# Two-layer block on one core: feed-forward weights of layer 1 in two transfers, the first feed-forward half ahead of the first value product, one pair of unread products moved

## The chip, the cores and the metric

The kernel runs on one core of one Trainium2 chip. The metric is the device time of one execution in microseconds; three executions of the kernel before took 355.24, 355.36 and 355.60 us, median 355.36.

## The reference

The input `x` is eight sequences of 256 tokens with 128 features, all float32. Two layers are computed, each as "normalise, then add an attention-like part and a feed-forward part".

```
xn = layernorm(x)
x  = x + attention0(xn) + moe0(xn)       # the change touches only this line
xn = layernorm(x)
x  = x + ssm1(xn) + ffn1(xn)
```

`attention0` has 16 query heads and 4 key/value heads of width 8, softmax over 256 keys, and an output product. `moe0` has eight logits per token (`xs @ Wg`); softmax, best two, weights divided by their sum. All experts share one pair of weights, so what is left is one gate number times `relu(xn @ w1) @ w2`, with `w1` 128x512 and `w2` 512x128. `ssm1` has an input product, a causal convolution of four taps, a gated scan over 16 states, and an output product. `ffn1` is a gated feed-forward net with two hidden 512x512 products.

The title's "layer 1" is the first of the two layers, which the code calls `layer0`.

## The kernel before

Every tensor stays in on-chip memory, 128 features or 128 tokens across the partitions. A batch is one sequence of 256 tokens, so there are eight batches in the first layer. The second layer works on four groups of 512 tokens.

Each of the five engines has a list of named steps written out by hand (`ORDERS`, line 72). The n-th occurrence of a name is the n-th call of the function of that name (`run_order`, line 127). An engine executes its list strictly in order; where a step needs something from another engine, it waits on a semaphore (`wait_ge`). Nothing reorders the steps at run time, so the place of a name in the string is the schedule.

Steps that matter here, with their lines:

- SyncE issues the transfers. At the start: `x_in` (line 361, three parts of `x`: 2, 6 and 8 tiles of 128 tokens), `head` (identity and query/key weights), `constants0` (output, value and gate weights, biases; called `cst`), `ffn_weights` (line 371, `w1` and `w2` side by side in the tile `w12`, 512 KB, one transfer). Then `put` and `put_keys` write query and key parts to DRAM, and `fetch` and `stack` read them back in another layout.
- TensorE: `xn_transposes` (line 502) turns a normalised batch, `project` (line 518) makes queries, and for the first batch a wide form of the keys, `project_keys` (line 525) makes keys, `v_gate` (line 493) makes values and gate logits, `ffn_in` (line 450) makes one half of the hidden layer of one batch (two 128-column blocks of `w1`, two steps per batch), `ffn_out` (line 464) multiplies the hidden layer with `w2`, `S` (line 381) makes scores for the row maxima, `A` makes the transposed scores for the softmax. A float32 product is recorded as two matmuls.
- `warm` (line 510) is a pair of bfloat16 products whose result nothing reads. There are 16 such pairs. They write to a bank that is otherwise unused then.
- ScalarE: `normalised` (line 553) scales `x`; `xn_out` (line 568) copies the transposed batch out of the accumulator bank, `own_keys` (line 612) masks the wide keys for the first four `S` steps; `relu` (line 579) empties an `ffn_in` bank.
- VectorE: `first_split` (line 758) cuts the first queries and keys into bfloat16 parts, `v_out` (line 698) empties the value product, `moments` (line 648) and `inverse` make the statistics, `M` (line 675) is the row maximum of one score step.

`v_gate` waits for the constants, for the transposed batch and for whatever last used its bank. For batch 0 that is written `q0` in `V_AFTER` (line 146): the query copy, the first part of `first_split`, and the wide query copy. `ffn_in` for batch 0 waits only for its weights and for the transposed batch (`-` in `F_AFTER`, line 150). It writes to a bank of its own, `bP`.

On TensorE the first steps stand in this order: eight `warm`, `xn_transposes`, two `warm`, `project`, `project_keys`, `warm`, `v_gate`, `ffn_in`, `xn_transposes`, `S`, `warm`, two `xn_transposes`, `S`, `project_keys`, `project`, two `S`, `ffn_in`, three `S`.

Of the kernel before, what the change touches and what calls it, by code (L numbers as in the profile page):

```python
# [27 lines left out]
DFF = 512  # L28
# [29 lines left out]
def reached(eng, sem, b, per, k):  # L58

    v = b * per + k  # L60
    if isinstance(v, int) and v <= 0:
        return
    eng.wait_ge(sem, v)


def settled(eng, sem, v):
# [3 lines left out]


ORDERS = dict(
    sync="""x_in head x_in constants0 x_in ffn_weights 2*put put_keys put 2*put_keys fetch 2*put_keys 2*put put_keys
        put fetch stack 3*put 3*rows stack fetch put_keys 2*put 2*rows put rows fetch 2*put put_keys loads stack
        2*rows put rows put_keys loads fetch stack 2*put 2*rows put rows fetch 3*put stack 3*rows fetch stack 2*put
        rows put 2*rows loads stack fetch 6*rows loads 3*b_rows out b_rows 7*out landed""",
    tensor="""8*warm xn_transposes 2*warm project project_keys warm v_gate ffn_in xn_transposes S warm 2*xn_transposes
        S project_keys project 2*S ffn_in 3*S 2*warm xn_transposes warm 3*S ffn_out S project 3*S ffn_in 2*S
        xn_transposes ffn_in max_rows 3*S v_gate warm 2*S ffn_out 2*S xn_transposes A S A S xn_transposes A S A S A
        project_keys S 2*A S project A S A 2*S ffn_in A S A S max_rows A S ffn_in v_gate A 2*S A S ffn_out A S project  # L80
        A S A S A S 2*pv A S A S A S pv A S A S A S pv A S A S max_rows heads A S A S v_gate pv A S A S back pv
# [77 lines left out]
def layer0(nc, sb, sem, banks, a, w, t, done):  # L159
# [11 lines left out]
    w12 = sb("w12", [P, 2 * DFF])  # L171
# [35 lines left out]

    X_PARTS = ((0, TPB), (TPB, 4 * TPB), (4 * TPB, NT))
    ld_x = [sem(f"ld_x{k}") for k in range(len(X_PARTS))]
    ld_head, ld_cst, ld_ffn = (sem(n) for n in ("ld_head", "ld_cst", "ld_ffn"))  # L210
    warm_end = sem("warm_end")
    spark_ok, warm_ok, kx_ok, own_ok, sc0_ok = (
        sem(n) for n in ("spark_ok", "warm_ok", "kx_ok", "own_ok", "sc0_ok"))
# [52 lines left out]
    def emptied(eng, before, n):  # L266

        name = before.split()[n]
        if name == "-":
            return  # L270
        for signal, per in EMPTIED[name[0]]:
            eng.wait_ge(signal, per * (int(name[1:]) + 1))
        if name == "q0":
            eng.wait_ge(q_split, 1)
            eng.wait_ge(qa_ok, 1)
# [7 lines left out]
    def sync_pieces(eng):  # L283
# [85 lines left out]
            eng.dma_start(cst[:, :], a["cst"]).then_inc(ld_cst, 16)  # L369

        def ffn_weights(n):
            eng.dma_start(w12[:, :], a["w12"]).then_inc(ld_ffn, 16)

        return dict(x_in=x_in, head=head, constants0=constants0, ffn_weights=ffn_weights, put=put, put_keys=put_keys, fetch=fetch, rows=rows,
                    stack=stack, loads=loads)


    def tensor_pieces(eng):
# [71 lines left out]
        def ffn_in(n):  # L450
            b, half = n // 2, n % 2
            if half == 0:
                eng.wait_ge(ld_ffn, 16)
                reached(eng, xnT_ok, b, 1, 1)
                emptied(eng, F_AFTER, b)
            else:
                reached(eng, h_ok, b, 2, 1)
            for j in range(2):
                c = 2 * half + j
                last = mm(bP[:, j * T:(j + 1) * T], w1[:, c * P:(c + 1) * P], xnT[b],  # L460
                          start=True, stop=True)
            last.then_inc(h_ps, 1)

        def ffn_out(b):
            reached(eng, h_ok, b, 2, 2)
            for q in range(TPB):
                for c in range(KC):
                    last = mm(bP[:, q * P:(q + 1) * P], hT[:, c, q * P:(q + 1) * P], w2[:, c, :],  # L468
                              start=(c == 0), stop=(c == KC - 1))
            last.then_inc(f_ps, 1)  # L470
# [54 lines left out]
        def project_keys(j):  # L525
# [6 lines left out]
            for i, b in enumerate(KEYS[j]):  # L532
                last = mm(key_bank(j)[32 * i:32 * i + 32, :], wk4[:, 0:NKV * HD], xnT[b], start=True, stop=True)
            last.then_inc(k_ps, 1)

        return dict(S=scores, A=attend_scores, pv=pv, heads=heads, ffn_in=ffn_in, ffn_out=ffn_out, back=back,
                    proj_out=proj_out, max_rows=max_rows, v_gate=v_gate, xn_transposes=xn_transposes,
                    project=project, project_keys=project_keys, warm=warm)
# [866 lines left out]
def program(nc, w, scr, out):  # L1405
    ctx = ExitStack()
    with ctx:
# [26 lines left out]
        with ExitStack() as only0:  # L1434
            pieces0 = layer0(nc, lambda name, shape, dt=F32: only0.enter_context(
                nc.sbuf_tensor(name, shape, dt)), sem, banks, a, w, t, done)
# [62 lines left out]
```

## Time and profile before

| quantity | value |
|---|---|
| three executions | 355.24, 355.36, 355.60 us, median 355.36 |
| the profiled execution | 355.43 us, of which the span is 353.6 us |
| TensorE busy | 343.7 us, 97% of the span |
| VectorE busy | 308.0 us, 87% |
| ScalarE busy | 287.8 us, 81% |
| GpSimd busy | 232.9 us, 66% |

The span reaches from the first to the last instruction of the five engines; 1.83 us of the profiled execution lie around it. Names in the rows: PE is TensorE, PEld its weight loads, DVE is VectorE, ACT is ScalarE, POOL is GpSimd, SPq is the queue of SyncE. L460 is line 460 of the kernel before. A row of the timeline gives start and length in microseconds, then engine, line, operation, operands, and how many instructions are merged in it. The bracket at the end is the idle time ahead of it and what ended that.

### The profile page before, as it was taken

How to read it: one execution, taken by the hardware profiler on the slowest of the kernel's cores; microseconds unless marked ns; L12 is line 12 of the kernel's file. 1: busy time of each engine (PE TensorE's matmuls, PEld its weight loads, DVE VectorE, ACT ScalarE, POOL GpSimd, SP SyncE). 2: the span in 40 equal slices, each digit the busy share in tenths (PEclk: the TensorE clock that was granted, in tenths of full speed). 3: DMA queues.
4: the chain of work that ended last, by engine and by line, in shares of the span. 5: the costliest groups of instructions: out<-in, count | busy, mean ns of one | idle time of the engine just before them, and what ended most of it. 6: DMA issues, size and time to landing. Idle time of an engine off the chain costs nothing.

```text
span 353.6 us, 5743 instructions
## 1 busy us (share of the span) xinstructions
PE 343.7 (97%) x1754; PEld 179.2 (51%) x1754; DVE 308.0 (87%) x530; ACT 287.8 (81%) x503; POOL 232.9 (66%) x294
## 2 busy tenths in 40 slices
PE   7999999999999999999999999999999999999996
PEld 4565634747565434434344446544455544555546
DVE  6899989989799798499999999999998978999840
ACT  3955886978688785899899969998999999689920
POOL 3553482332720201346997979999999989999990
PEclk9999999999999999999999999999999999999999
DMA  6449477936447003000000000000000000000000
GB/s 228 114 124 184 84 200 172 157 91 135 93 136 123 4 2 122 22 1 2 22 0 3 1 0 24 0 15 2 0 13 26 1 30 2 1 0 1 2 30 30
DMA packets 29198, 19.39 MB, mean 55 GB/s; under 512 B 4256, under 2 KB 28144, under 8 KB 28912
## 3 DMA queue, kind: packets, MB, share of 16 engines
q1 hardware_dynamic: 29168, 19.03, 22.4%
q8 instruction: 14, 0.23, 0.3%
q14 instruction: 16, 0.13, 0.1%
HBM read 13.45 MB, written 5.37 MB: 53 GB/s over the span
## 4 chain that ended last, share of the span: by engine, by line
PE 87%; DVE 6%; ACT 3%; issue 2%; POOL 1%; ACTq 0%; DVEq 0%; POOLq 0%
PE bank L1027 16%; PE bank L1016 15%; PE bank L436 7%; PE bank L423 4%; PE bank L1098 4%; PE bank L1051 4%; DVE mx L681 4%; PE bank L460 4%; PE bank L990 4%; PE bank L1071 4%; PE bank L468 4%; PE bank L1006 4%; PE bank L1007 4%; PE bank L400 3%; PE bank L1088 2%
## 5 line engine op out<-in xcount | busy, mean ns | idle before, releaser
L1367 POOL TENSOR_TENSOR acc<-acc,hb 128x512 f32<-128x512 f32 x128 | 158.3, 1267 | 16.5 <-DVE hb L1311 16.4
L1311 DVE TENSOR_TENSOR_SCAN hb<-da,bank 128x512 f32<-128x512 f32 x128 | 146.0, 1201 | 8.7 <-PE bank L990 8.1
L681 DVE TENSOR_REDUCE mx<-bank 128x2 f32<-128x512 f32 x128 | 81.6, 681 | 7.3 <-PE bank L400 4.8
L1216 ACT ACTIVATE da<-dt,nega 128x510 f32<-128x510 f32 x128 | 81.3, 709 | 0.1
L1016 PE MATMUL bank<-sil,ld 128*128 128x512 f32 x128 | 59.2, 592 | 0.0
L1027 PE MATMUL bank<-gelu,ld 128*128 128x512 f32 x128 | 58.4, 592 | 0.0
L631 ACT ACTIVATE pt<-bank 128x512 f32<-128x512 f32 x72 | 39.8, 599 | 7.0 <-PE bank L436 4.2
L423 PE MATMUL bank<-q_st,k_st 51*128 51x512 bf16 (+1 forms) x128 | 38.8, 381 | 0.5 <-ACT pt L631 0.5
L400 PE MATMUL bank<-k_st,q_st 48*128 48x256 bf16 x248 | 38.1, 272 | 0.3 <-DVE mx L681 0.2
L1027 PEld LDWEIGHTS bank<-gelu,ld 128*128 128x128 f32 x128 | 24.1, 190 | 26.0 <-issue 25.2
L1016 PEld LDWEIGHTS bank<-sil,ld 128*128 128x128 f32 x128 | 23.9, 190 | 23.2 <-issue 22.2
L631 ACT ACTIVATE hb<-bank 128x512 f32<-128x512 f32 x56 | 30.8, 595 | 5.1 <-PE bank L423 4.9
L990 PE MATMUL bank<-b_parts,sel 96*128 96x512 bf16 x64 | 23.4, 381 | 0.3 <-DVE hb L1311 0.3
L400 PEld LDWEIGHTS bank<-k_st,q_st 48*128 48x128 bf16 x248 | 17.6, 94 | 8.6 <-DVE mx L681 4.5
L423 PEld LDWEIGHTS bank<-q_st,k_st 51*128 51x128 bf16 (+1 forms) x128 | 9.2, 94 | 25.0 <-ACT pt L631 13.8
L846 POOL TENSOR_TENSOR m_parts<-negm,m_parts 32x128 bf16<-32x128 f32 x8 | 3.3, 417 | 24.9 <-ACT negm L577 24.9
L1098 PEld LDWEIGHTS bank<-ld,gelu 128*128 128x128 f32 x128 | 16.4, 192 | 4.5 <-issue 4.2
L1280 DVE SCALAR_TENSOR_TENSOR xc<-bank,ld,xc 128x510 f32<-128x510 f32 (+2 forms) x24 | 17.7, 741 | 0.7
L436 PE MATMUL bank<-pt,v_sb 128*32 128x512 f32 x144 | 17.9, 600 | 0.2 <-issue 0.2
L460 PE MATMUL bank<-xnT,w 128*128 128x256 f32 x64 | 17.5, 396 | 0.4 <-DVE on L693 0.4
L1204 ACT ACTIVATE gelu<-bank,ld 128x512 f32<-128x512 f32 x14 | 9.1, 687 | 9.4 <-PE bank L1027 9.4
L1006 PE MATMUL bank<-xnT,ld 128*128 128x512 f32 x32 | 16.5, 598 | 0.2 <-DVE mx L681 0.2
(166 smaller groups left out, 537.7 us busy)
## 6 DMA issues: line engine op xcount, KB each, us to landing
q_st<-q_scr SPq DMA_DIRECT2D x15, 192.0 KB, 3.8
q_st<-q_scr SPq DMA_DIRECT2D x7, 384.0 KB, 5.0
ld<-in_pack SPq DMA_DIRECT2D x2, 1024.0 KB, 5.6
q_scr<-qk_parts SPq DMA_DIRECT2D x8, 192.0 KB, 2.6
k_st<-k_scr SPq DMA_DIRECT2D x14, 96.0 KB, 4.7
q_scr<-qk_parts SPq DMA_DIRECT2D x8, 128.0 KB, 1.8
out<-x SPq DMA_DIRECT2D x8, 128.0 KB, 1.9
ld<-in_pack SPq DMA_DIRECT2D x1, 968.0 KB, 6.0
```

The costliest lines, as they stand in the source:

```text
L400: last = mm(score_bank(b, n)[:, j * T:(j + 1) * T], q_st[b % 2][0:ROWS, 2 * pair + j, q * P:(q + 1) * P], k_st[b % 2][0:ROWS, 2 * pair // ...
L423: mm(st(b, n)[:, :], k_st[b % 2][lo:, kv, kt * P:(kt + 1) * P], q_st[b % 2][lo:, h0:h0 + 2, :].rearrange("r h n -> r (h n)"), start=True, ...
L436: last = mm(bP[kv * VW:(kv + 1) * VW, :], v_sb[b % NV][:, kt, kv, at:at + VW], prob(b, 4 * grp + kv), start=(grp == 0), stop=(grp == 3))
L460: last = mm(bP[:, j * T:(j + 1) * T], w1[:, c * P:(c + 1) * P], xnT[b], start=True, stop=True)
L631: act(prob(b, n), st(b, n)[:, :], ACT.Exp, scale=HD ** -0.5).then_inc(p_ok, 1)
L681: eng.tensor_reduce(mx[:, 2 * pair:2 * pair + 2, q], score_bank(b, n)[:, :].rearrange("p (h k) -> p h k", h=2), AX.X, ALU.max).then_inc(mx ...
L990: mm(b_bank(g, s)[:, :], sel[:, s, :], b_parts[:, g % 2, :], start=True, stop=True).then_inc(b_ps, 1)
L1016: last = mm(f_bank(g, c)[:, :], h1[:, k, c * P:(c + 1) * P], sil[:, k, :], start=(k == 0), stop=(k == KC - 1))
L1027: last = mm(f_bank(g, c)[:, :], h2[:, k, c * P:(c + 1) * P], g2[:, k, :], start=(k == 0), stop=(k == KC - 1))
L1216: act(da(n)[:, :, 1:T], dt[:, g % 2, c, :].rearrange("p (b n) -> p b n", b=GB)[:, :, 1:T], ACT.Exp, scale=nega[:, c, s:s + 1]).then_inc(da ...
L1311: eng.tensor_tensor_scan(hb[:, s % NPAIR, c, :], da(n).rearrange("p b n -> p (b n)"), b_bank(g, s)[:, :], 0.0, ALU.mult, ALU.add).then_inc ...
L1367: TT(acc[:, g % 2, c, :], acc[:, g % 2, c, :], hb[:, s % NPAIR, c, :], ALU.add).then_inc(add_ok, 1)
```

## The change

The weights `w12` come in two transfers of 256 KB with a semaphore each: `w1` is issued ahead of the third part of `x`, `w2` behind it. `ffn_in` waits for the first, `ffn_out` for the second (a new wait, eight times in all). On TensorE the first `ffn_in` goes ahead of the first `v_gate`, and the pair of unread products that stood ahead of `v_gate` goes to behind the first `S`, where there are two pairs then. All other steps keep their places, and the same bytes, products and copies are executed.

```diff
-    sync="""x_in head x_in constants0 x_in ffn_weights 2*put put_keys put ...
+    sync="""x_in head x_in constants0 ffn_weights x_in ffn_weights 2*put put_keys put ...
-    tensor="""8*warm xn_transposes 2*warm project project_keys warm v_gate ffn_in xn_transposes S warm 2*xn_transposes
-        S project_keys project 2*S ffn_in 3*S ...
+    tensor="""8*warm xn_transposes 2*warm project project_keys ffn_in v_gate xn_transposes S 2*warm 2*xn_transposes S
+        project_keys project 2*S ffn_in 3*S ...
...
-    ld_head, ld_cst, ld_ffn = (sem(n) for n in ("ld_head", "ld_cst", "ld_ffn"))
+    ld_head, ld_cst = (sem(n) for n in ("ld_head", "ld_cst"))
+    ld_ffn = [sem(f"ld_ffn{k}") for k in range(2)]
...
         def ffn_weights(n):
-            eng.dma_start(w12[:, :], a["w12"]).then_inc(ld_ffn, 16)
+            c = slice(n * DFF, (n + 1) * DFF)
+            eng.dma_start(w12[:, c], a["w12"][:, c]).then_inc(ld_ffn[n], 16)
...
             if half == 0:
-                eng.wait_ge(ld_ffn, 16)
+                eng.wait_ge(ld_ffn[0], 16)
...
         def ffn_out(b):
+            eng.wait_ge(ld_ffn[1], 16)
             reached(eng, h_ok, b, 2, 2)
```

## Rows read from the trace of the kernel before

**Rows 1.** The page: busy time of TensorE, its granted clock by slice, the chain's shares.
```profile
PE 343.7 (97%) x1754; PEld 179.2 (51%) x1754; DVE 308.0 (87%) x530; ACT 287.8 (81%) x503; POOL 232.9 (66%) x294
...
PEclk9999999999999999999999999999999999999999
...
PE 87%; DVE 6%; ACT 3%; issue 2%; POOL 1%; ACTq 0%; DVEq 0%; POOLq 0%
```

**Rows 2.** The chain of waits in order of time, 9 to 30 us: start, length, what.
```profile
11.69 0.77 ACT xn L560 x2
...
12.90 0.41 PE bank L507 x2
```

**Rows 3.** Timeline of TensorE, 8 to 13 us.
```profile
8.11 0.39 PE L514 MATMUL bank<-warm_in 128*128 128x256 bf16 x2
...
9.16 0.61 PE L498 MATMUL bank<-cst,xnT 128*128 128x40 f32 x4 [0.65 <-DVE qk_rest L762]
9.60 1.11 PE L460 MATMUL bank<-xnT,w 128*128 128x256 f32 x4
...
10.54 0.38 PE L507 MATMUL bank<-head,xn 128*128 128x128 f32 x2
10.80 1.10 PE L389 MATMUL bank<-hb,dt 128*128 128x512 f32 x2
...
11.74 0.38 PE L514 MATMUL bank<-warm_in 128*128 128x256 bf16 x2
...
11.96 0.38 PE L507 MATMUL bank<-head,xn 128*128 128x128 f32 x2
```

**Rows 4.** DMA issues on SyncE's queue, issues by size with time to landing, two stretches.
```profile
2.56 0.43 SPq L363 DMA_DIRECT2D x_sb<-in_x  x1
3.04 0.43 SPq L372 DMA_DIRECT2D w<-in_w  x1
...
x_sb<-in_x SPq DMA_DIRECT2D x1, 512.0 KB, 5.5
w<-in_w SPq DMA_DIRECT2D x1, 512.0 KB, 6.2
...
6.00:7.00 1.00, 0.87 (x6) 0.58 (x5) 0.96 (x10) 0.38 (x1) 0.00 (x0) 1.00 0.96 373
7.00:8.00 1.00, 1.00 (x5) 0.34 (x4) 0.80 (x6) 0.38 (x2) 0.00 (x0) 1.00 0.79 320
```

**Rows 5.** Timeline of VectorE, 8 to 12 us.
```profile
8.42 0.48 DVE L762 SCALAR_TENSOR_TENSOR qk_rest<-bank,cst,qk_parts 128x256 f32<-128x256 f32 x1 [0.33 <-ACT qk_parts L595]
...
9.90 0.23 DVE L706 TENSOR_TENSOR v_sb<-bank,cst 128x64 f32<-128x64 f32 x1 [0.21 <-PE bank L498]
...
11.35 1.62 DVE L652 BATCH_NORM_STATS2 bst<-x_sb 128x6 f32<-128x128 f32 x8
```

**Rows 6.** Timeline of ScalarE, 9 to 17 us.
```profile
9.77 0.89 ACT L616 ACTIVATE hb<-dt,cst 128x256 f32<-128x256 f32 x2
...
12.37 0.38 ACT L570 ACTIVATE xnT<-bank 128x256 f32<-128x256 f32 x1
...
14.87 0.47 ACT L604 ACTIVATE qk<-bank,cst 96x256 f32<-96x256 f32 x1
...
16.32 0.60 ACT L583 ACTIVATE hT<-bank 128x512 f32<-128x512 f32 x1
```

**Rows 7.** Timeline: unread products at the start and at 18.8 us.
```profile
1.86 3.59 PE L514 MATMUL bank<-warm_in 128*128 128x256 bf16 x16 [1.86 <-DVE warm_in L641]
...
18.79 0.61 PE L514 MATMUL bank<-warm_in 128*128 128x256 bf16 x4
```

**Rows 8.** Timeline: weight loads behind a wait; then line 468 (`ffn_out`), its idle time.
```profile
12.87 0.20 PEld L507 LDWEIGHTS bank<-head,xn 128*128 128x128 f32 x2 [0.77 <-issue]
...
20.72 1.86 PEld L468 LDWEIGHTS bank<-w,hT 128*128 128x128 f32 x16 [0.21 <-ACT hT L583]
...
  ACT hT L583: 1.0, 4
```

More of the change, by code:

```diff
@@ L72 @@
 ORDERS = dict(
[L73 to L76, printed above, removed]
-    tensor="""8*warm xn_transposes 2*warm project project_keys warm v_gate ffn_in xn_transposes S warm 2*xn_transposes
-        S project_keys project 2*S ffn_in 3*S 2*warm xn_transposes warm 3*S ffn_out S project 3*S ffn_in 2*S
+    sync="""x_in head x_in constants0 ffn_weights x_in ffn_weights 2*put put_keys put 2*put_keys fetch 2*put_keys
+        2*put put_keys put fetch stack 3*put 3*rows stack fetch put_keys 2*put 2*rows put rows fetch 2*put put_keys
+        loads stack 2*rows put rows put_keys loads fetch stack 2*put 2*rows put rows fetch 3*put stack 3*rows fetch
+        stack 2*put rows put 2*rows loads stack fetch 6*rows loads 3*b_rows out b_rows 7*out landed""",
+    tensor="""8*warm xn_transposes 2*warm project project_keys ffn_in v_gate xn_transposes S 2*warm 2*xn_transposes S
+        project_keys project 2*S ffn_in 3*S 2*warm xn_transposes warm 3*S ffn_out S project 3*S ffn_in 2*S
         xn_transposes ffn_in max_rows 3*S v_gate warm 2*S ffn_out 2*S xn_transposes A S A S xn_transposes A S A S A
```

## The prediction

> **What bounds the kernel now.** I read the page first. TensorE is busy 97% of the span and carries 87% of the chain that ended last, and its granted clock is full in all forty slices [rows 1]. So an edit on TensorE's list counts if it moves the products that follow it, and an edit on another queue counts if TensorE or its partner waits for it. Then the chain in order of time, around the edit: it does not run through TensorE's early products. It runs on ScalarE (the last piece shown is the scaling of a batch at 11.69 and the copy behind it), and enters TensorE at 12.90 with the transposes of batch 3 [rows 2]. From there its pieces are TensorE's in one unbroken row to the second value product near 28 us. The timeline of TensorE tells why: there are holes ahead of 12.90, one of 0.65 us ahead of `v_gate` (released by VectorE's first split) and one of about 0.5 us ahead of 12.90 itself [rows 2, 3]. The question is whether the change fills a hole that anyone waits behind.
>
> **Transfers.** In the queue, `w1` takes the place of the third part of `x` (issued 2.56) and that part takes the place of the weights (3.04) [rows 4]. In the kernel before, 512 KB issued at 2.56 landed at 2.56 + 5.5 = 8.06, and 512 KB issued at 3.04 at 9.24. `w1` is half as large. At the 320 to 373 GB/s of these stretches the missing 256 KB are 0.70 to 0.82 us, so `w1` lands at about 7.3; the bounds are that and 8.06. TensorE asks for it at 8.11, where the unread pair starts now [rows 3]. The third part of `x` lands 0.7 to 0.8 later, about 8.8, and at the latest at 9.24 by the place of the old weights; its reader, the statistics of VectorE, comes at 11.35 [rows 4, 5]: 2.1 us or more of cover. `w2` has the same bytes ahead of it as before and is read at 20.72 [rows 8]. The additional issue costs SyncE 0.43 us from 3.5 to 3.9, and its first `put` depends on the first query copy, long after. Cost of all this: 0. If the cover were gone (`w1` landing at 8.5, say), `ffn_in` and `v_gate` would be late; that is a rival below.
>
> **`ffn_in` ahead of `v_gate`.** It takes TensorE from 9.60 to 10.54, 0.94 us [rows 3]. Started at 8.11 it is through at 9.05. `v_gate` is released by VectorE at 8.42 + 0.48 = 8.90 and started at 9.16 [rows 3, 5]; it still starts at 9.16, and VectorE's `v_out` stays at 9.90. So the hole is filled at no cost to the value product (0 to 0.1 if the slack of 0.11 is lost). What is gained is that TensorE is through at 9.60 and not at 10.54. Next are the transposes of batch 1, for which ScalarE is ready about 9.9; they are 0.6 early, but ScalarE copies them out only at 11.4, behind its own list. Then `S`, which needs the masked keys: 9.77 + 0.89 = 10.66 [rows 6]. Transposes released by a ScalarE copy at 12.37 + 0.38 = 12.75 start at 12.90, 0.15 later [rows 2, 6]. By that lag `S` may start at 10.81; it starts at 10.80 now [rows 3]. The gain at `S` is therefore 0, with 0.14 (10.66 itself) as the other end. The first hidden half isn't read before `relu` at 16.32, which stands behind other work on ScalarE [rows 6]: nothing is gained there either. The time of the hole has moved to 9.6 to 10.8.
>
> **The unread pair.** Four unread products take 0.61 us and two 0.39 [rows 3, 7], so one costs 0.11 and the pair 0.22. In its old place it stood in the hole and cost nothing. In its new place it stands between the first `S` and the transposes of batch 2, which start at 11.96 and end at 12.34; ScalarE's copy of them starts at 12.37 [rows 3, 6]. Now they end at 12.56. The chain names ScalarE's own scaling, up to 12.46, as what released that copy [rows 2], so 0.09 may be hidden: the copy, and with it the transposes of batch 3 at 12.90, come 0.13 to 0.22 late; with the 0.14 of the last part taken off, 0 to 0.22. I take 0.2 at 12.90, as the two rows that end at 12.34 and start at 12.37 are the nearer ones.
>
> **How far it goes.** From 12.90 on TensorE's row is unbroken, so what is added there is passed on. ScalarE runs beside it with small slack: its key copy starts at 14.87, and its `relu` ends at 16.92, where the second `ffn_in` starts. The first `ffn_out` at 20.72 waited 0.21 for `relu` [rows 8], which ends a row of ScalarE's work that TensorE's lateness hardly reaches. There I take off about half of the shift, leaving 0.12. Behind it the two engines take turns, and I let 0.12 stand to the end. Bounds: 0 and 0.22.
>
> **The new wait.** `ffn_out` gets one further wait, eight times, for a transfer that landed long ago. Queued behind it are its sixteen matmuls, and VectorE's gated sum waits for those. The trace has no row for a satisfied wait. The nearest: `v_gate` starts 0.26 behind its releaser with another wait to be processed after that, and the transposes of batch 3 start 0.15 behind theirs, with none; the difference is 0.11 [rows 3, 5, 6]. Eight of them are 0.88 us. But the new wait stands ahead of the one for `relu`, and is done while TensorE still works on what it has or waits for `relu` (1.0 us in four of the eight cases) [rows 8]. I take 0; bounds 0 and 0.9.
>
> **Sum.** 0 (transfers) + 0 (order of `ffn_in` and `v_gate`) + 0.12 (pair) + 0 (waits) = +0.12. On the profiled execution, 353.6 of span and 1.83 around it, that is 355.55. That execution is 0.07 above the median of the runs, so for a median 355.48. I forecast 355.5. About 0.2%, 0.7 us, is what a measurement of this kernel can tell from no change, so this is "no change".
>
> **Rivals.**
>
> *TensorE's early list does set the chain.* If ScalarE's first copies or the keys are not what `S` waits for, the filled hole of 0.65 is gained, less the 0.12: 355.36 - 0.53 = 354.8. For it: the hole is real, and everything behind 12.90 hangs on TensorE. Against it: ScalarE's rows from 9.77 on leave no room, and the chain names ScalarE. Chance 0.07. If the hole were worth something more because a whole later turn of the engines is caught earlier, 354.5: 0.03.
>
> *`w1` lands late.* If the transfers are served side by side and not in the order of issue, `w1` may land with the third part of `x`, around 8.5. Then `ffn_in` runs from 8.6 to 9.55, `v_gate` starts 0.4 late, and VectorE's row of splits and statistics with it; with the pair that is 355.36 + 0.4 = 355.8, as the later `ffn_out` takes off little. Against it: each of the two large transfers landed in order, 1.18 apart. Chance 0.1. In this case the change does not do what it says, as the half meant to fill the hole makes another.
>
> *The new wait is paid on the path.* Place: each of the eight `ffn_out` steps; price 0.11 each; with the 0.12 that gives 355.36 + 0.88 + 0.12 = 356.36, slower. It decides from the point at which `ffn_out` finds TensorE's queue empty and `relu` long done. Half of the eight have no wait for `relu` in the rows, but TensorE works through there. Chance 0.05; half of it paid, 355.9, is within the range.
>
> *TensorE's clock falls.* The holes of the list move to 9.6 to 10.8. The unread products ran at 0.22 us each at the start (3.59 us for sixteen), which is the lower level of 1.2 GHz, and at 0.11 later, 2.4 GHz, though the granted clock is full in every slice [rows 1, 7]. Had the clock to climb again, the products from 10.8 to about 14.4 would take twice as long: about +3.5, 359. Against it: two holes as long as the new ones were passed at 2.4 GHz, and no products are taken out. Chance 0.03.
> The Trainium skill bears on this ("TensorE: Matmul & The Clock Gate", Part 1): the throttled clock is the default, and recent activity releases it. It is the rule that speaks against moving unread work away from the start. By the rule the sum would be 359 only if the activity before 10.8 fell; this change raises it at 8.5 to 9.1 and lowers it at 9.6 to 10.8, and the trace has no row at that pattern.
>
> **Chances and range.** The forecast with its bounds (355.3 to 355.7) has 0.68, a late `w1` 0.1, half a wait paid 0.04, faster ways 0.1, paid waits 0.05, the clock 0.03. The range 354.9 to 356.0 holds the forecast, the late `w1` and half-paid waits and reaches to the first of the faster ways; it leaves out the full price of the waits and the clock. Faster by over 0.2% (under 354.65): 0.06, counting half of the first rival's surroundings. Slower by over 0.2% (over 356.07): 0.08. Within: 0.86.
>
> **What would show it.** Right: `ffn_in` starts at 8.1 and `v_gate` at 9.16; a hole of about 0.4 ahead of the transposes of batch 1 and another ahead of `S`, which starts at 10.8 again; four unread products behind `S`; the transposes of batch 3 at 13.1 and not 12.90; the same 0.1 at the first `ffn_out` (20.8) and at the second value product. The third part of `x` lands before 9.3. Wrong: `S` before 10.6, or `v_gate` after 9.3; an idle time of TensorE in front of `ffn_out` in the column of idle time that was not there; unread products or score products at twice their length behind 10.8; a shift at 20 us that is gone or has grown at 120 us.

## The result: 0.98 us slower in the first nine executions, outside the range

Nine executions of each kernel on one chip: changed 356.34 us median (356.05 to 356.54), before 355.36 (355.24 to 355.73), ratio (of the means) 1.0023 with a 95% interval of 1.0013 to 1.0034. Here and below, a few executions of 500 to 1970 us, of before and of changed kernels alike, are left out, the profiled one of `same_again` among them. I had forecast 355.5 in a range of 354.9 to 356.0. The profiled execution of the changed kernel took 356.34 us with a span of 354.5, 0.9 longer than that of before.

The page of the changed kernel (busy time and shares; the clock by slice; the chain's shares), against [rows 1]:

```profile
PE 344.7 (97%) x1754; PEld 180.1 (51%) x1754; DVE 308.0 (87%) x530; ACT 287.7 (81%) x503; POOL 232.7 (66%) x294
...
PEclk9999999999999999999999999999999999999999
...
PE 88%; DVE 6%; issue 2%; ACT 2%; POOL 1%; DVEq 0%; POOLq 0%; ACTq 0%
```

TensorE has the same 1754 products and is busy 1.0 us longer; the other engines haven't changed. So nothing was added but time on TensorE's row, and the chain has moved 1% from ScalarE to it. Where? The timeline of TensorE after the change, 5 to 13.6 us, against [rows 3]:

```profile
5.35 0.66 PE L510 MATMUL bank<-head,xn 128*128 128x128 f32 x2
5.81 1.06 PE L517 MATMUL bank<-warm_in 128*128 128x256 bf16 x4
6.66 0.96 PE L524 MATMUL bank<-xnT,head 128*128 128x256 f32 x2
...
8.53 1.13 PE L462 MATMUL bank<-xnT,w 128*128 128x256 f32 x4
9.58 0.61 PE L501 MATMUL bank<-cst,xnT 128*128 128x40 f32 x4
10.85 0.41 PE L510 MATMUL bank<-head,xn 128*128 128x128 f32 x2 [0.66 <-DVE srt L715]
11.22 1.10 PE L391 MATMUL bank<-hb,dt 128*128 128x512 f32 x2
12.16 0.60 PE L517 MATMUL bank<-warm_in 128*128 128x256 bf16 x4
12.59 0.38 PE L510 MATMUL bank<-head,xn 128*128 128x128 f32 x2
13.54 0.41 PE L510 MATMUL bank<-head,xn 128*128 128x128 f32 x2 [0.56 <-ACT xnT L573]
```

Compared line by line with before, the shift has three parts.

- **At 8.5 us: +0.42**, before any moved step has run. `v_gate` starts at 9.58 against 9.16, the first `S` at 11.22 against 10.80.
- **At 12.6 us: +0.21 more.** Four unread products stand behind the first `S` where there were two, and the transposes of batch 2 are 0.63 late, those of batch 3 (12.90 before) 0.64.
- **Between 67 and 103 us: +0.25 more.** The shift stays 0.64 past the first three `ffn_out` (20.72 before, 21.35 now) and then grows in small steps at four later ones, to 0.89. From there it is constant to the end.

The sum, 0.89, is the difference of the spans. The chain after the change now runs over the value product, VectorE's emptying of it and the transposes of batch 1, in place of ScalarE's scaling [rows 2]; here 8.6 to 13.6 us of it in order of time:

```profile
8.60 1.06 PE bank L462 x4
9.66 0.54 PE bank L501 x4
...
10.32 0.22 DVE v_sb L709
10.55 0.17 DVE srt L715 x2
10.71 0.14 issue
10.85 0.41 PE bank L510 x2
11.26 1.06 PE bank L391 x2
12.32 0.44 PE bank L517 x4
12.76 0.23 PE bank L510 x2
12.99 0.02 issue
13.01 0.39 ACT xnT L573
```

The 0.44 of the unread products (`L517 x4`) is a piece of the chain. That is the plain sign of a loss.

### The profile page after: what moved, and what is told of

It is laid out like the page before. It is cut to its first block, busy times and chain, and to the rows that moved or that the text cites. A ratio compares the mean times of both kernels' runs of the same rounds, so it can differ in the third digit from the quotient of the medians.

```text
span 354.5 us, 5752 instructions
## 1 busy us (share of the span) xinstructions
PE 344.7 (97%) x1754; PEld 180.1 (51%) x1754; DVE 308.0 (87%) x530; ACT 287.7 (81%) x503; POOL 232.7 (66%) x294
## 4 chain that ended last, share of the span: by engine, by line
PE 88%; DVE 6%; issue 2%; ACT 2%; POOL 1%; DVEq 0%; POOLq 0%; ACTq 0%
PE bank L1030 16%; PE bank L1019 15%; PE bank L438 7%; PE bank L425 4%; PE bank L462 4%; PE bank L1054 4%; PE bank L1101 4%; DVE mx L684 4%; PE bank L993 4%; PE bank L1074 4%; PE bank L471 4%; PE bank L1009 4%; PE bank L1010 4%; PE bank L402 3%; PE bank L1091 2%
## 5 line engine op out<-in xcount | busy, mean ns | idle before, releaser
L684 DVE TENSOR_REDUCE mx<-bank 128x2 f32<-128x512 f32 x128 | 81.6, 682 | 7.6 <-PE bank L402 4.8
```

Of the source, the lines that this page charges most:

```text
L684: eng.tensor_reduce(mx[:, 2 * pair:2 * pair + 2, q], score_bank(b, n)[:, :].rearrange("p (h k) -> p h k", h=2), AX.X, ALU.max).then_inc(mx ...
```

## The experiments

Each was timed in five rounds, beside the kernel before on the same chip; `same_look` and `changed_look` are one profiled execution each. Because single executions of the unchanged kernel spread over more than 1 us, I give the mean beside the median. By their times alone `pair_alone` and `pair_in_the_hole` can't be told from no change, as their intervals hold 1, and `transfers_alone` barely; what they cost is shown by the profiles. A shift below is the start of a TensorE instruction minus the start of the same one in the profile of before.

| kernel | n | median | mean | lowest | before beside it: median, mean, lowest | ratio, 95% interval |
|---|---|---|---|---|---|---|
| changed (first) | 9 | 356.34 | 356.29 | 356.05 | 355.36, 355.46, 355.24 | 1.0013 to 1.0034 |
| same_again | 10 | 355.41 | 355.50 | 355.23 | 355.51, 355.58, 355.19 | 0.9990 to 1.0009 |
| transfers_alone | 10 | 355.85 | 355.92 | 355.51 | the same | 1.0000 to 1.0019 |
| pair_alone | 11 | 355.84 | 355.83 | 355.47 | the same | 0.9999 to 1.0016 |
| one_wait | 11 | 355.73 | 355.87 | 355.59 | the same | 1.0001 to 1.0019 |
| changed_again | 11 | 356.24 | 356.19 | 355.76 | 355.61, 355.69, 355.26 | 1.0001 to 1.0019 |
| pair_in_the_hole | 11 | 356.08 | 356.02 | 355.67 | the same | 0.9999 to 1.0016 |
| hole_and_one_wait | 11 | 355.51 | 355.67 | 355.26 | the same | 0.9990 to 1.0009 |
| more_waits | 11 | 356.06 | 356.19 | 355.73 | 355.67, 355.76, 355.33 | 1.0003 to 1.0021 |
| early_unread | 11 | 355.45 | 355.53 | 355.29 | the same | 0.9983 to 1.0001 |
| early_again | 11 | 355.48 | 355.50 | 355.27 | 355.38, 355.47, 355.22 | 0.9992 to 1.0010 |

**same_again and same_look: the kernel before, unchanged.**

> The kernel before, unchanged, against itself. The profiles of before and after differ by 0.42 us ahead of 8 us already: in the one of before the products come at the faster spacing from about 5.2 us, in the one of after only from about 7.3 us. Theory A (the moment at which TensorE's clock rises differs from execution to execution of any kernel, whatever its code): median 355.4 within 0.15, and the profile may show the faster spacing at another moment than 5.2 us, with the whole span longer or shorter by up to 0.5 us. Theory B (the change itself delays that moment): 355.4 too, and the profile shows 5.2 us again.

> One look at the kernel before, for the moment at which its products come at the faster spacing. Theory A: anywhere from 5 to 7.6 us, and everything behind it shifted by up to 0.6 us against the first profile. Theory B (the moment belongs to the kernel's code): 5.2 us again.

same_again has no profile that can be used. same_look took 355.29 us, and its products have the faster spacing early, as in the first profile. That doesn't settle the question of the start; the profiles of the other kernels do, below. What the timing gives is the spread: in all sessions together 103 executions of before, 355.19 to 356.65, mean 355.62. The first three, on which the case rested, had a mean of 355.40.

**transfers_alone: the halves, the semaphores and the new wait; TensorE's list as before.**

```diff
     # the changed kernel, with the tensor list of before
+    ... project project_keys warm v_gate ffn_in xn_transposes S warm 2*xn_transposes S ...
```

> Only the transfers are changed (two halves, two semaphores, the wait ahead of every second feed-forward half); TensorE's list is the old one. Theory A (three separate costs: 0.22 for the unread pair, 0.06 for each of four new waits that lie on the path, and the rest of the 0.98 from the start of the kernel): +0.25 us from the waits, 355.6, with steps of 0.06 near 67, 82, 88 and 102 us. Theory B (the transfers cause the late clock as well): +0.25 and +0.42, 356.0, and the faster spacing from about 7.3 us. Rival C (the four steps come from the shifted queries and keys and not from the wait): 355.4, no steps.

Mean +0.34 (0.32 by the lowest). The profile has no late start: the first input lands 0.17 earlier than in the profile of before, and everything is 0.17 early until the first, second and third `ffn_out`. Then the shift grows at four of the eight: it is -0.09 behind the `ffn_out` of 67 us, -0.02 behind that of 82, +0.04 behind that of 88 and +0.09 behind that of 102 us, and stays there. The row at one of them, the weight loads of TensorE from 81 us, of before:

```profile
81.06 0.31 PEld L400 LDWEIGHTS bank<-k_st,q_st 48*128 48x128 bf16 x3
81.58 0.09 PEld L490 LDWEIGHTS bank<-head,mx 128*32 128x32 f32 x1 [0.21 <-issue]
81.58 1.88 PEld L468 LDWEIGHTS bank<-w,hT 128*128 128x128 f32 x16
```

and of transfers_alone:

```profile
80.97 0.31 PEld L402 LDWEIGHTS bank<-k_st,q_st 48*128 48x128 bf16 x3
81.50 0.09 PEld L493 LDWEIGHTS bank<-head,mx 128*32 128x32 f32 x1 [0.21 <-issue]
81.58 1.86 PEld L471 LDWEIGHTS bank<-w,hT 128*128 128x128 f32 x16
```

In before, the first load of `ffn_out` (L468) follows the load of `max_rows` (L490) at once, both at 81.58. With the wait between them it comes 0.08 later. ScalarE's `relu` had been done at 81.08 in before and 81.00 here, so it isn't that. It is the same at 67 us. At 88 and 102 us it is not: there `relu` ends last. The rows at 88 us, of before and then of transfers_alone (`relu` is the row of ScalarE, which ends at 88.30 and 88.28):

```profile
87.70 0.60 ACT L583 ACTIVATE hT<-bank 128x512 f32<-128x512 f32 x1
88.35 1.75 PEld L468 LDWEIGHTS bank<-w,hT 128*128 128x128 f32 x15 [0.21 <-ACT hT L583]
...
87.68 0.60 ACT L586 ACTIVATE hT<-bank 128x512 f32<-128x512 f32 x1
88.39 1.75 PEld L471 LDWEIGHTS bank<-w,hT 128*128 128x128 f32 x15 [0.27 <-issue]
```

The load comes 0.06 behind the end of `relu` in before and 0.11 with the new wait. The trace's records of semaphore instructions, which the timeline leaves out, tell what the wait is. In before `ffn_out` has no such record of its own: its one wait stands on its first weight load. With a second wait each `ffn_out` has one, of 0.05 us, on line 63 (the wait for `relu`, in the helper `reached`), and at 67, 82, 88 and 102 us alike the load starts 0.08 behind the start of that record. The page counts the same: 5743 instructions in before, 5752 here and in the changed kernel, which is eight such records and one more transfer. Theory A holds, rival C falls. The late clock did not come with the transfers here, so B falls for them as far as one profile tells; changed_again has them too and starts early.

**pair_alone: the unread pair moved, nothing else.**

```diff
-    ... project_keys warm v_gate ffn_in xn_transposes S warm 2*xn_transposes ...
+    ... project_keys v_gate ffn_in xn_transposes S 2*warm 2*xn_transposes ...
```

> Only the unread pair is moved: from ahead of the first value product to behind the first score product, the first feed-forward half stays behind the value product, one transfer. Theory A: the transposes of batch 2 start 0.22 later, and nothing takes that up: +0.22, 355.58. Theory B (moving unread work away from 8.1 us delays the rise of the clock): not possible by order of time, as the rise lies ahead of 8.1 us in both profiles; so it also says +0.22. My recorded forecast said +0.12, with about half absorbed at the first second half at 20.7 us.

Mean +0.25, lowest +0.28. The profile is 0.59 late at 7.04 us and 0.81 at 12.90: the pair costs 0.22, and the shift is still 0.80 in the last row. No part is absorbed at 20.7 us or later. Its start is the telling thing, because up to 8.1 us this kernel's lists are those of before, word for word:

```profile
5.42 0.66 PE L507 MATMUL bank<-head,xn 128*128 128x128 f32 x2
5.87 1.06 PE L514 MATMUL bank<-warm_in 128*128 128x256 bf16 x4
6.72 1.07 PE L521 MATMUL bank<-xnT,head 128*128 128x256 f32 x2
7.63 0.59 PE L523 MATMUL bank<-xnT,head 128*128 128x256 f32 x2
```

In the profile of before:

```profile
5.80 0.60 PE L514 MATMUL bank<-warm_in 128*128 128x256 bf16 x4
6.53 0.67 PE L521 MATMUL bank<-xnT,head 128*128 128x256 f32 x2
```

The same four unread products take 0.60 us there and 1.06 here. That is 0.11 and 0.21 apart from one to the next: the 2.4 GHz and the 1.2 GHz level. The views write a granted clock of 1.00 for both stretches, but that is not a reading: the trace's first record of the clock, which says 1.0, begins at 5.34 us in before and at 7.62 in pair_alone, each time where the spacing changes (7.34 in the first profile of the changed kernel), and ahead of it there is none.

**one_wait: the changed kernel, the new wait ahead of the first `ffn_out` only.**

```diff
         def ffn_out(b):
-            eng.wait_ge(ld_ffn[1], 16)
+            if b == 0:
+                eng.wait_ge(ld_ffn[1], 16)
```

> The changed kernel, but the wait for the second half of the weights stands ahead of the first ffn_out only, and not of the other seven. Theory A: the four steps of 0.06 near 70, 83, 90 and 102 us go: 0.25 faster than the changed kernel, 356.1. Rival C (the steps are not the wait's): as the changed kernel, 356.35. In both the pair costs 0.22 still.

Mean +0.29 over before, where the changed kernel has +0.83 and +0.50. Its profile is 0.29 late at 12.90 and 0.26 to 0.28 late from there to the end, with no step between 60 and 110 us. Taking the wait away takes the steps away.

**changed_again and changed_look: the changed kernel, unchanged.**

> The changed kernel, unchanged. Theory A (pair 0.22, four or five satisfied waits on the path together 0.26, and a clock that rises at another moment in each execution): the first nine executions, 0.98 above before, had more late rises than their share; now +0.5 us, 356.0, with single times from 355.7 to 356.5. Theory D (the combination costs more than its parts, which is 0.98 against 0.37 for the transfers alone and 0.32 for the pair alone): +0.98 again, 356.5. The profile: steps of 0.06 to 0.14 between 67 and 102 us as in the first one, the start by chance.

> One more look at the changed kernel, for the moment of the rise and for what else differs from execution to execution. Theory A: from 8 us to the end +0.48 over before plus what the start gives; steps at 12, 67, 82, 88, 102 us.

Median +0.63, mean +0.50: theory A's value, and not the 0.98 of D. Lowest 355.76, where the first nine had nothing below 356.05. The two profiles differ in what is accidental and agree in what is the change's:

| shift against the profile of before | first profile | changed_again | changed_look | what |
|---|---|---|---|---|
| near 7.3 us | +0.42 | -0.03 | +0.37 | moment of the clock, landing of `x` |
| from there to 15 us | +0.22 | +0.22 | +0.23 | the pair |
| from there to 105 us | +0.25 | +0.26 | +0.33 | the waits |
| from there to the end | 0 | +0.36 | -0.01 | a pause at 121 us |
| sum | +0.89 | +0.81 | +0.92 | |

The pause of changed_again, in the timeline of TensorE:

```profile
120.47 0.39 PE L402 MATMUL bank<-k_st,q_st 48*128 48x256 bf16 x2
121.17 0.37 PE L425 MATMUL bank<-q_st,k_st 51*128 51x512 bf16 x1 [0.31 <-issue]
```

In before, the corresponding two start at 120.03 and 120.25. No engine released the second one; the idle time is put down to "issue". What held TensorE's queue there isn't visible, and no other profile has it.

**pair_in_the_hole: the moved pair ahead of the transposes of batch 1, in TensorE's new hole.**

```diff
-    ... ffn_in v_gate xn_transposes S 2*warm 2*xn_transposes ...
+    ... ffn_in v_gate warm xn_transposes S warm 2*xn_transposes ...
```

> The changed kernel with the moved pair of unread products put between the first v_gate and the transposes of batch 1, where TensorE sat idle 0.66 us in the changed kernel; one pair only stays behind the first score product. Theory A: the 0.22 goes, the waits stay: +0.26 over before. The first score product stands as before at 0.14 behind the masked keys. My recorded forecast would have it at 0.12 less than the changed kernel.

Mean +0.33, 0.17 less than changed_again beside it; the profile shows no step at 12 us and ends 0.35 late, of which 0.27 come between 67 and 104 us.

**hole_and_one_wait: both repairs.**

```diff
-    ... ffn_in v_gate xn_transposes S 2*warm 2*xn_transposes ...
+    ... ffn_in v_gate warm xn_transposes S warm 2*xn_transposes ...
...
+            if b == 0:
                 eng.wait_ge(ld_ffn[1], 16)
```

> Both repairs: the pair in the hole, and the wait for the second half of the weights ahead of the first ffn_out only. Theory A: 0, equal to the kernel before within 0.1, as the first feed-forward half ahead of the value product gains nothing: the transposes of batch 1 wait for the value product's emptying, and the first scores for the masked keys. Rival E (the filled hole of 0.65 is worth something once its costs are taken away): 355.0 or less.

Mean -0.02, ratio 1.0000. What remains of the change here is the order of `ffn_in` and `v_gate` and the two transfers. The interval leaves some 0.3 us either way, but the profile leaves less: the shift is 0.05 when `v_gate` starts and 0.09 at the end. So it is worth nothing, neither way, and rival E, which asked for 355.0 or less, falls. The timeline of TensorE tells why it isn't a gain:

```profile
8.16 1.13 PE L462 MATMUL bank<-xnT,w 128*128 128x256 f32 x4
9.21 0.61 PE L502 MATMUL bank<-cst,xnT 128*128 128x40 f32 x4
9.65 0.39 PE L518 MATMUL bank<-warm_in 128*128 128x256 bf16 x2
10.48 0.41 PE L511 MATMUL bank<-head,xn 128*128 128x128 f32 x2 [0.44 <-DVE srt L716]
10.85 1.10 PE L391 MATMUL bank<-hb,dt 128*128 128x512 f32 x2
```

`ffn_in` fills the old hole, and the hole reopens at 9.9, ended by VectorE's `MAX8` (`srt`). The transposes start at 10.48 (10.54 in before) and `S` at 10.85 (10.80).

**more_waits: the kernel before with three satisfied waits ahead of each `ffn_out`.**

```diff
         def ffn_out(b):
+            for _ in range(3):
+                eng.wait_ge(ld_ffn, 16)
             reached(eng, h_ok, b, 2, 2)
```

> The kernel before with three waits for the feed-forward weights, long landed, ahead of each ffn_out, and nothing else: the disputed cost three times over. Theory A (a satisfied wait takes TensorE's queue about 0.06 us, and is on the path where the row of score products ends and ffn_out is next): steps of about 0.2 at 82, 88 and 102 us and some at 67; with the 0.26 of one wait as the measure 0.6 to 0.8 over before, 356.2. Rival F (waits for one semaphore are folded, or the queue runs ahead of them): +0.26 or less.

Mean +0.43, median +0.39. In the profile the shift goes from -0.17 at the start to +0.30 behind the last `ffn_out`: 0.47, between A's 0.6 to 0.8 and F's 0.26. At 81.6 us the three waits bring the first load 0.20 behind that of `max_rows`, where one cost 0.08. The rows there, and then those at 88 us:

```profile
81.60 0.09 PEld L492 LDWEIGHTS bank<-head,mx 128*32 128x32 f32 x1 [0.21 <-issue]
81.80 1.86 PEld L470 LDWEIGHTS bank<-w,hT 128*128 128x128 f32 x16
...
87.89 0.60 ACT L585 ACTIVATE hT<-bank 128x512 f32<-128x512 f32 x1
88.61 1.53 PEld L470 LDWEIGHTS bank<-w,hT 128*128 128x128 f32 x13 [0.27 <-issue]
```

Three times one would be 0.24, and they are not three: the page counts 5759 instructions, 16 more than before, so the three waits became two instructions in each `ffn_out`. At 67 and 82 us, where `relu` had ended 0.5 us earlier, both are paid (steps of 0.17 and 0.18). At 88 and 102 us `relu` ends last, at 88.49 here, and the load comes 0.11 behind it, just as with one added wait: the first of the two instructions is done while TensorE waits for `relu`, and only the one that holds the wait for `relu` is left, a step of 0.06. So an instruction that only waits costs 0.06 to 0.11 where it is exposed, and a further one ahead of it costs nothing where `relu` ends last.

**early_unread and early_again: unread products from 1.30 us and not 1.86.**

```diff
         def ones(n):
+            eng.memset(warm_in[:, :], 1.0).then_inc(warm_ok, 1)
             eng.memset(spark[:, :], 1.0).then_inc(spark_ok, 1)
             eng.memset(t["eps"][:, :], LN_EPS).then_inc(spark_ok, 1)
-            eng.memset(warm_in[:, :], 1.0).then_inc(warm_ok, 1)
...
-    tensor="""8*warm ...      vector="""clear_values ones clear_values ...
+    tensor="""10*warm ...     vector="""ones clear_values clear_values ...
```

> The kernel before, but VectorE fills the operand of the unread products first of all, so that they start near 1.35 and not at 1.86 us, with ten pairs of them at the start and not eight. Nothing else differs. Theory A (the rise of the clock comes some time after TensorE has begun to work, by chance sooner or later): in more executions the rise lies ahead of the first useful product; median 355.3 and the slow tail (up to 356.4 in before) shorter, mean 0.1 to 0.3 lower. Rival G (the rise does not depend on the start of the work): as before, or 0.1 slower where the 20 unread products at the slower spacing reach 5.6 us.

> The kernel with the earlier and longer row of unread products once more. Eleven executions gave 355.29 to 355.84, mean 355.53, beside a kernel before with a mean of 355.76 and a tail up to 356.65; the interval just touched 1. Theory A: mean again 0.1 to 0.3 lower and no execution above 356.0. Rival G: a mean within 0.05 of before and a tail like its.

The first session gave a mean 0.23 lower than before, the second 0.03 higher. In the second, before itself had a mean of 355.47 only. Together 22 executions lie between 355.27 and 355.84, and none is above 356, where 15 of the 103 of before are. That fits a shorter tail; a lower median isn't shown. In both profiles the products are at the faster spacing when the first useful one comes. But in early_again that is only from 5.5 us on, later than in the profile of before, though the work started 0.56 earlier: an earlier start did not bring an earlier rise there, and rival G isn't excluded. The rows of early_unread, whose twenty products end at 5.04:

```profile
1.30 3.74 PE L514 MATMUL bank<-warm_in 128*128 128x256 bf16 x20 [1.30 <-DVE warm_in L639]
5.39 0.41 PE L507 MATMUL bank<-head,xn 128*128 128x128 f32 x2 [0.35 <-DVE xn L667]
```

## Why the prediction was wrong, step by step

**The new wait: the step that failed most.** The prediction set the price well enough (0.11 from two lags in the rows; measured 0.06 to 0.08), and then multiplied it by 0, because it "stands ahead of the one for `relu`, and is done while TensorE still works on what it has". That holds at the first three `ffn_out` and, in the profiles, at the last. It fails at the four near 67, 82, 88 and 102 us. At 67 and 82 the weight loads of `ffn_out` follow the previous load at once, `relu` having ended 0.5 us earlier, so an instruction more in the queue is on the path. At 88 and 102 `relu` does end last, but the wait for it has become an instruction of its own, and the load comes 0.11 behind `relu` where it came 0.06 behind it. For 67 and 82 the trace of before had said so: idle time stands ahead of six of the eight (1.0 us in four, 0.4 in two) and not ahead of these two, and the chain went through TensorE. A row of products with nothing idle between them was read as cover, when it was the path. Measured: 0.25 to 0.26 in the profiles, +0.34 in the mean of transfers_alone. It was a rival with the right mechanism, a price of 0.88 and a chance of 0.05. That its sum, 356.36, is nearly the 356.34 of the first nine is luck: the waits cost 0.26, and the rest has other causes.

**The pair: right mechanism, half the size.** The row price of 0.22 and the place were right. The step that failed is "there I take off about half of the shift". The reason given, that ScalarE's `relu` ends TensorE's wait at 20.72, was wrong twice. `relu` ended at 20.45, 0.27 ahead of the load, while the load at 88.35 came 0.06 behind `relu`; and at 20.72, 29.55 and 42.04 alike the load starts 0.31 behind the previous one, whether `relu` ended 0.27, 1.08 or 0.43 us before. The bracket at 20.72 [rows 8] names `relu` only as the last wait. And ScalarE's row starts with the copies that TensorE's late transposes release, so `relu` came 0.64 late as well (21.09 in the changed kernel, the load at 21.35): the two engines shift together. All five profiles that pay for the moved pair keep 0.19 to 0.23 of it past the first `ffn_out`.

**The start: missed as a cause, and not the change's.** The +0.42 ahead of 8 us in the first profile is the moment at which TensorE goes from 1.2 to 2.4 GHz, less 0.20 by which the first product came earlier. pair_alone shows it late with the very instructions of before, and changed_again shows it early with those of the change. The prediction treated the clock only as a thing that might fall; the row of sixteen unread products at some 0.22 each [rows 7] would have allowed the question of when it rises. The Trainium skill describes it ("TensorE: Matmul & The Clock Gate", Part 1: one kernel shows different numbers of slow products at its start in different runs, and it puts the penalty at under 1% of a typical span); the profiles agree, with 0 to 0.7 us, at most 0.2% of the span here.

**The transfers, and the order of `ffn_in` and `v_gate`: right.** `ffn_in` did not wait for `w1`; the two halves landed 4.6 and 5.9 us after their issues. In the undelayed profiles `ffn_in` starts at 8.1 to 8.2 and `v_gate` at 9.1 to 9.2, and the filled hole is worth 0 (hole_and_one_wait). One reason was incomplete: I had the transposes of batch 1 ready about 9.9, behind ScalarE's scaling. They also wait for VectorE's reading of the value product, `v0` in `X_AFTER` ("- v0 x1 x2 ..."), and so start at 10.5. That the masked keys stand behind it at 10.7 made the outcome the same.

**The sum.** Pair 0.22 and waits 0.26 are 0.48, which would have been 355.84, inside the range and "within 0.2%". The two terms that failed were 0.36 too small together; they alone don't carry the time out of the range. Measured: +0.98 by the medians of the first nine, +0.50 by the means of the next eleven. Over all, 20 executions of the changed kernel have a mean of 356.23 and 103 of before 355.62, a difference of 0.61. The 0.13 beyond 0.48 are within what late starts and a pause can do, which is not shown further. Whether the changed kernel has more of these than before is not settled: two of its three profiles started late, and neither of the two of before. The first nine of before were on the low side as well (mean 355.46 against 355.62).

## What to carry to other kernels

A wait for something that landed long ago is free only where the engine's queue has time to process it. In `ffn_out` the only wait stood on the first weight load; a second one became an instruction of its own, which cost 0.06 to 0.08 us at four of eight places. Put such a wait once, ahead of the first use, and not into a step that is repeated, and compare the instruction counts of the two pages to see what was added. When a filler is moved, it is free only in front of a wait, so look again for the hole after the other step has been moved: the hole had gone from ahead of `v_gate` to behind it. Before trusting a difference of 0.2%, time the unchanged kernel against itself in several sessions, and split the difference of two profiles into where it arises, as a list of shifts in order of time.

## What was not expected of the hardware

- The moment at which products go to the faster spacing varied from 4.6 us (transfers_alone) to 7.6 (pair_alone) among profiles whose TensorE steps are the same up to there, and moved all that followed by up to 0.7 us. The views write 1.00 throughout; the distance of equal products (0.21 and 0.11 us) shows it, and so does the start of the trace's first clock record, where there is one (transfers_alone and early_unread have none).
- The first 128 KB of `x` landed 2.7 us after the issue in the first profile and in pair_in_the_hole and 2.5 in the others, which moves the first useful product by 0.1 to 0.2.
- One pause of TensorE's queue, +0.36 us at 121 us, in one of the twelve profiles that can be set against that of before.
- Satisfied waits: at 81.6 us one added wait delays the load by 0.08 us and three, as two instructions, by 0.20. Where `relu` ends last, the load comes 0.06 us behind it with the wait on the load and 0.11 with the wait as an instruction of its own, whether one wait was added or three.
